# Attention and mixture-of-experts kernel on one core: how many groups of turned probability blocks stand in front of the small scores

## The reference, cut to what matters

```python
x = x + layernorm(attn(layernorm(x)))
x = x + layernorm(ffn(layernorm(x)))

# attn
q, k = rope(h @ Wq), rope(h @ Wk);  v = h @ Wv
scores = einsum('bkgqd,bkpd->bkgqp', q, k) * D ** -0.5
scores = where(causal, scores, -1e30)
probs = softmax(scores)
out = einsum('bkgqp,bkpd->bkgqd', probs, v) @ Wo
```

## Time and profile before

| what | value |
|---|---|
| device time, median of 3 runs | 1429.14 us (1427.6 to 1429.7) |
| the profiled execution: its own time | 1428.59 us |
| its span in the trace | 1426.5 us |
| granted TensorE clock, mean | 0.992 |
| PE busy | 1316.9 us (92%) |
| PEld busy | 925.0 us (65%) |
| DVE busy | 978.3 us (69%) |
| ACT busy | 778.0 us (55%) |
| POOL busy | 409.5 us (29%) |

### The profile page before, as it was taken

The page is one execution under the profiler, slowest core; times in us unless marked ns, Lnnn a source line. Parts: engine busy times, 40 slices in busy tenths (PEclk is TensorE's granted clock), DMA queues, the critical chain, the costliest instruction groups (busy, mean ns, idle before and its releaser), DMA issues.

```text
span 1426.5 us, 31016 instructions
## 1 busy us (share of the span) xinstructions
PE 1316.9 (92%) x10432; PEld 925.0 (65%) x10432; DVE 978.3 (69%) x2044; ACT 778.0 (55%) x1709; POOL 409.5 (29%) x412
## 2 busy tenths in 40 slices
PE   2699999999999999999999989999998999999996
PEld 1477777777777776877777777777776644444442
DVE  2777777765777778477777875777776366666665
ACT  2566666655666666466666655666664233333333
POOL 0343444422443434243444322443420000000000
PEclk9899999999999999999999999999999999999999
DMA  8211112111212121112112011212110000000000
GB/s 245 85 39 63 66 48 67 42 60 35 68 48 70 37 71 53 42 39 71 59 51 74 31 60 35 68 48 70 37 53 1 1 1 8 8 7 8 8 8 15
DMA packets 79028, 67.64 MB, mean 47 GB/s; under 512 B 39904, under 2 KB 62304, under 8 KB 78816
## 3 DMA queue, kind: packets, MB, share of 16 engines
q1 hardware_dynamic: 78944, 66.55, 14.3%
HBM read 7.81 MB, written 2.10 MB: 7 GB/s over the span
## 4 chain that ended last, share of the span: by engine, by line
PE 66%; DVE 12%; issue 9%; ACT 8%; SPq 2%; DMA 2%; POOL 1%; DVEq 0%; ACTq 0%; POOLq 0%
PE rows L434 15%; PE o_out L483 12%; PE turn L453 8%; PE rows L623 7%; DVE neg_max L1058 5%; ACT probs L728 4%; PE o_out L646 3%; PE rows L437 3%; PE proj_bank L453 3%; PE o_out L402 2%; PE proj_bank L402 2%; DMA turned<-raw 1%; PE proj_bank L385 1%; PE proj_bank L387 1%; PE proj_bank L386 1%
## 5 line engine op out<-in xcount | busy, mean ns | idle before, releaser
L728 ACT ACTIVATE probs<-rows,neg_max 128x768 f32<-128x768 f32 (+7 forms) x512 | 375.0, 737 | 246.6 <-DVE neg_max L1058 242.0
L1058 DVE TENSOR_REDUCE neg_max<-rows 128x1 f32<-128x768 f32 (+7 forms) x512 | 363.4, 751 | 114.7 <-PE rows L437 114.6
L483 PE MATMUL o_out<-probsT,v_g 128*64 128x128 f32 (+1 forms) x3328 | 278.2, 317 | 0.7 <-DVE probsT L1072 0.7
L483 PEld LDWEIGHTS o_out<-probsT,v_g 128*64 128x64 f32 x3328 | 201.3, 137 | 68.3 <-issue 19.3
L453 PE MATMUL turn<-cf,probs 128*128 128x128 f32 x1792 | 239.5, 274 | 1.3 <-DVE probsT L1072 1.1
L737 ACT ACTIVATE probsT<-turn 128x512 f32<-128x512 f32 x256 | 152.7, 596 | 111.4 <-PE turn L453 107.6
L434 PE MATMUL rows<-kk,qh 64*128 64x512 f32 (+2 forms) x768 | 164.8, 425 | 48.1 <-ACT probs L728 42.6
L453 PEld LDWEIGHTS turn<-cf,probs 128*128 128x128 f32 x1792 | 192.2, 141 | 1.9 <-DVE probsT L1072 1.3
L1072 DVE COPY probsT<-turn 128x512 f32<-128x512 f32 x256 | 174.6, 682 | 1.4 <-PE turn L453 1.1
L919 POOL TENSOR_TENSOR turned<-turned,cf 128x512 f32<-128x512 f32 x96 | 122.9, 1281 | 170.6 <-DMA turned<-raw 170.6
L928 POOL COPY inv_wide<-inv_sum 128x256 f32<-128x256 f32 x128 | 52.4, 409 | 415.6 <-DVE inv_sum L1064 387.4
(11 more groups left out here) (154 smaller groups left out, 1682.7 us busy)
## 6 DMA issues: line engine op xcount, KB each, us to landing
turned<-raw SPq DMA_DIRECT2D x192, 128.0 KB, 2.0
kk<-kk SPq DMA_DIRECT2D x16, 512.0 KB, 2.9
kl<-kl SPq DMA_DIRECT2D x16, 512.0 KB, 3.7
v_g<-v_all SPq DMA_DIRECT2D x32, 256.0 KB, 3.0
slab_a<-w_qk SPq DMA_DIRECT2D x16, 256.0 KB, 2.6
xm<-in_x SPq DMA_DIRECT2D x4, 512.0 KB, 7.3
slab_b<-w_qk SPq DMA_DIRECT2D x16, 128.0 KB, 2.2
out<-xm SPq DMA_DIRECT2D x8, 256.0 KB, 2.3
```

Of the source, the lines that this page charges most:

```text
L483: ins = mm(dst, v_g[p][:, t, :], x, start=t == 0, stop=t == big_w - 1)
L728: A(probs[:, s % 2, q * 128:q * 128 + width], rows[h][:, 0:width], ACT.Exp, bias=neg_max[:, s % 2, item:item + 1], accum_out=exp_sum[:, s ...
L1058: V.tensor_reduce(neg_max[:, s % 2, item:item + 1], rows[h][:, 0:width], AX_X, ALU.max, negate=True).then_inc(max_ready, 1)
```

## The change

`groups_first(s, last)` gives the number of groups of turned blocks that stand in front of the small scores: 4 in steps 0 and 4, 2 in step 7 and in step 2 (but not in the last group of a batch), and 3 in the others, as before. PE's two loops over the groups use it. DVE's order follows: with four groups in front, the copy of group 3 comes behind `keep_outputs` and ahead of the small maxima; with two, the copy of group 2 comes behind the small maxima, ahead of the copy of group 3. The wait for the copy of group 2 at the end of PE's step stays where it is. No instruction is added or removed, and ACT's, POOL's and SP's queues are as before.

```diff
+def groups_first(s, last):
+
+    return 4 if s % STEPS_P == 0 else 2 if s == STEPS_G - 1 or s == 2 and not last else 3
...
                 if depth > 0:
-                    for j in range(3):
+                    for j in range(groups_first(s, last)):
                         turn_probs(b, g1, s1, j, last and s > 2)
...
                 score_rows(b, g, s, 0)
                 if depth > 0:
-                    for j in range(3, MOVES):
-                        turn_probs(b, g1, s1, j)
+                    for j in range(groups_first(s, last), MOVES):
+                        turn_probs(b, g1, s1, j, last and s > 2)
                     turn_kept(pe, step_index(b, g1, s1), 2)
...
                 row_maxima(b, g, s, 1)
                 if depth > 0:
                     keep_turned(b, g1, s1, 1)
-                    keep_turned(b, g1, s1, 2)
+                    if groups_first(s, last) > 2:
+                        keep_turned(b, g1, s1, 2)
                 if depth > 1:
                     keep_outputs(b, *earlier(g, s, 2))
+                if depth > 0 and groups_first(s, last) > 3:
+                    keep_turned(b, g1, s1, 3)
                 if last and s == 2 and b + 1 < B:
                     split_tokens(b + 1, 0, proj_bank)
                 row_maxima(b, g, s, 0)
                 if depth > 0:
-                    keep_turned(b, g1, s1, 3)
+                    if groups_first(s, last) < 3:
+                        keep_turned(b, g1, s1, 2)
+                    if groups_first(s, last) < 4:
+                        keep_turned(b, g1, s1, 3)
```

## The result

| | before | after |
|---|---|---|
| median | 1429.73 us (1427.39 to 1433.74, 20 runs) | 1427.34 us (1425.55 to 1430.15, 20 runs) |
| profiled execution | 1428.59 us | 1427.37 us |
| its span | 1426.5 us | 1425.3 us |
| mean granted TensorE clock | 0.992 | 0.986 |
| DVE busy | 978.3 us | 971.4 us |

The ratio is 0.9984, with an interval of 0.9977 to 0.9991: 2.4 us faster, 0.17%. The forecast was 1422.5 us, 0.45% faster. The direction is right and the time lies within the range of 1415 to 1429, but the gain is 2.4 us where the forecast's sum had 6.4.

The account below looks back on a forecast made before the run. The prediction took PE as the bound, with time won only in its waits, chiefly for ACT's exponentials. Terms of -6.0, -2.4, +1.0 and +1 gave -6.4 us against 1428.59, forecast 1422.5 us; 8-in-10 range 1415 to 1429.

Parts of the forecast that it names:

- The bound: Whole kernel: PE holds 66% of the chain; time is won only where PE idles, mainly waiting for ACT's exponentials, 42.6 us.
- A group is worth 0.44: PE's turned blocks: a group of four transposes takes 0.44 us, so moving it shifts PE's later work by at most that.
- Steps 7 and 0: Each change of group: step 0's small-score wait of 0.64 is covered, PE waits for group 2's copy instead; -0.50 us, 12 times.
- Steps 2 and 3: End of step 2 into step 3: the same with smaller numbers, second part of big scores at 459.2, not 459.29; -0.2 us, 12 times.
- Steps 4 and 5: Step 4's wait of 0.21 is covered, but later small maxima delay step 5's exponentials; +0.08 us, 13 times.
- The irregular places: Last groups, batch changes and the end: about +2 us, less about 1 us in the last groups' step 4; net +1 us.
- The sum: Whole kernel: -6.0, -2.4, +1.0 and +1 make -6.4 us; forecast 1422.5 us, 0.45% faster.
- give 1419 to 1428: Bounds from PE's restart (0 to 0.3 us at 24 places), group 3's bank (0 to 0.2) and irregular places (-1 to +4).
- The copy is no bound: Rival, ends of steps 7 and 2: group 2's copy is done before PE asks; another -6 us, 1416.5; chance 0.15.
- The new wait costs more than it saves: Rival, ends of steps 2 and 7: PE restarts 0.4 to 0.6 after the copy; 1434 at 0.5 lost each; chance 0.12.
- Step 0 keeps nothing: Rival: later small maxima use up the 0.2 slack before step 1, step 4 loses 0.3; 1427 to 1429; chance 0.06.
- Simply covered: Rival, steps 0, 3 and 4: all four waits before scores go, 1.7 us a group; 1402; chance 0.04.

## Why the prediction was right in its mechanism and wrong in its size

- **The bound.** Right. In a regular group PE's idle time before the scores fell from 1.70 to 1.42 us, and three waits are left of four. A wait costs more than its idle time: from the first to the second part of step 0's big scores it was 1.40 us with 0.43 of idle time (435.12 to 436.52), and 0.80 without a wait (435.22 to 436.02), so 0.17 are the restart, for which the prediction took 0.1. 0.28 of idle time and one restart are 0.45, and a regular group became 0.44 shorter (-0.36 - 0.15 + 0.07).
- **A group is worth 0.44.** Right. From step 0's first transpose to the outputs it was 1.41 us with twelve (437.53 to 438.94) and is 1.96 with sixteen (436.94 to 438.90): 0.55 more, where 0.44 and 0.05 to 0.15 for the bank were forecast. The some 275 ns that the Trainium skill ("TensorE: Matmul & The Clock Gate", Part 4) gives for a 128x128 bf16 transpose within a kernel agree with the recorded duration of one here (in fp32, 275 ns in the mean). As the cost of each to PE they would make the sixteen 4.4 us, and the starts do not show that.
- **Steps 7 and 0: -0.50 forecast, -0.36 measured.** The step that failed is "with it, at about 435.9 (0.05 to 0.12 after the copy's end)". The copy itself came as forecast, 2.37 behind the small scores (2.38 forecast). But PE was on its way 0.26 after its end: 3.31 behind the small scores and not 3.16. No row of the kernel before had shown PE's restart behind a wait for DVE. Those 0.15 stay to the end, since no slack follows until step 1's second part: step 0's small scores came 0.09 later than before (441.00 + 0.84 against 441.75), where 0.05 sooner was forecast. The rest of the working held: the outputs' start, the covered wait of 0.64, and step 1's second part not waiting though the small maxima came 0.44 later (0.29 forecast).
- **Steps 2 and 3: -0.20 forecast, -0.15 measured.** The same step: the restart came 0.15 after the copy's end and not 0.1.
- **Steps 4 and 5: +0.08 forecast, +0.07 measured.** Right in its mechanism, which two runs showed: without the fourth group 4+5 is 15.27, and with the copy of group 3 behind the small maxima 15.09.
- **The irregular places: +1 forecast.** In the undisturbed program they come to about +0.7: the last groups' step 4 gave 0.43 each in three batches (-1.0 with the 0.27 that the last batch gives back in step 5, as forecast), the three changes of batch cost 0.05, 0.32 and 0.40, together 0.8 and not 2, the first group's steps 2 and 3 came out at +0.2 and not -0.2, since the prediction took them for regular (+0.4), and a few single steps make +0.5.
- **The sum.** 12 times -0.36, 12 times -0.15 and 13 times +0.07 are -5.2, where the same terms were -7.4 in the prediction; with the irregular places the undisturbed program stands at about -4.5 against -6.4. The profiles themselves differ by 1.6 us, so 4.8 of the 6.4 are missing in them. Of these, 1.9 us are in mis-sized terms, PE's restart behind the new wait first of all. The larger part is a **term that the sum did not have**: it took for granted that all that is not in the steps it names stays as it is. That cost 2.9 us more than before in the profiles: 0.8 in the first three steps with their low clock, 1.8 in late steps elsewhere, 0.3 ahead of the steps and behind them. Why the late steps grow is shown at one place (less slack behind a late landing); whether the clock at the start goes with the change stays open. The bounds "give 1419 to 1428" left all this out as well: that the time lies within them is luck, helped by their width. Two slips of arithmetic are small beside it: 1422.2 and 0.55 are 1422.7 and not 1422.5, and the parts of the bounds, added straight, reach from about 1417 to 1431.
- **The rivals.** *The copy is no bound* is refuted by its 16.7 us of waits and by the wait moved. *The new wait costs more than it saves* was the right mechanism with the wrong price: it decides from a restart 0.27 later than forecast, and 0.15 and 0.05 were measured. It is true in part, though, at each change of group: there the two groups in front cost 0.08 on top of the four. *Step 0 keeps nothing* fell, since step 1's second part never waited. *Simply covered* fell: of 1.70 us of idle time per regular group only 0.28 went.

## What to carry to other kernels

Moving cover in front of a wait moves the end of that cover too: ask which semaphore wait at the end of the step was always early, and is last now. Here that wait stood in front of work that did not need it, and moving it to its true user was worth more (9.5 us between the two medians) than the whole change (2.4 us). Test the parts of a change alone: four groups in front were worth more without the two.

A sum over regular steps is what the undisturbed program gains. How late steps and a low clock answer to it needs several profiles of both kernels. The shortest length of each step is a good figure to compare with such a sum, as long as neighbouring steps do not trade time with one another: check the first steps of a loop by their sum. And look at the first round of a loop as at the last: a step may wait there for something else than in the regular rounds.

## What the runs showed of the hardware

- **The first steps' time is not one number.** The same instructions of steps 0 and 1 took 17.27 to 19.88 us in nine plain profiles and 14.84 when PE's gaps were filled. The granted clock was at its lower level in two or three stretches there (38.7 to 49.0 and 52.4 to 55.8 us in the first profile of before; 37.8 to 48.0, 51.4 to 58.2 and 61.7 to 65.1 in that of after), in or behind gaps of PE (2.81 us before 39.34 and 3.77 before 52.15 in the one; 3.08 before 38.95, 3.77 before 51.76 and 1.71 before 60.87 in the other). The Trainium skill ("TensorE: Matmul & The Clock Gate", Part 1) says that the number of matmuls at the low clock at a kernel's start is run-variable for the same kernel. The traces agree: the low stretches within the first 70 us add up to 13.7 us in every plain profile of before and to 13.7, 13.7, 17.1, 17.1 and 20.5 in those of after. Whether the changed kernel falls into the longer stretches more often stays open: its steps 0 and 1 took over 17.9 us in four profiles of five, those of the kernel before in none of four, but of the variants with the whole change one had 17.30 (the wait moved) and three 18.27 to 19.78.
- **Filling gaps with unread products gained 4.7 to 6.5 us** in three kernels (1429.2 to 1424.5, 1426.5 to 1420.9, 1416.6 to 1410.2), for 69 added products at the start and the end.
- **A restart behind a wait has no one price.** From the end of the same copy of 0.68 us to PE's first matmul it was 0.24 us at the changes of group in batch 0, 0.27 in the other batches, 0.15 behind step 2, and 0.06 at the three changes of batch, each to 0.01 us within the changed kernel's first profile. Why they differ wasn't tried.
